# Two transformer layers with routed experts on one core: the routed work cut into 16 tiles of 512 rows and 6 of 256, and the last normalisations dealt out in small steps

## The reference, cut to what matters

```python
x = x + _layernorm(attention_1(_layernorm(x)))               # 8 sequences of 512 rows, 512 columns
y = _layernorm(x)
h = y + attention_2(rmsnorm(y, ln1_w))
z = rmsnorm(h, ln2_w)
shared = (silu(z @ sh_gate) * (z @ sh_up) / 8) @ sh_down     # 512 -> 256 -> 512
probs = sigmoid(z @ router_w + router_b)                     # 7 routed experts
scores, idx = top_k(probs, 2); scores = scores / sum(scores)
combined = sum over e in 0..6 of w[..., e] * expert_ffn(z, r_gate[e], r_up[e], r_down[e])
x = x + _layernorm(h + shared + combined)
```

## Time and profile before

| | us |
|---|---|
| runs (3) | median 2325.95, 2321.92 to 2331.52 |
| the profiled execution's own time | 2323.38 |
| its span, first to last instruction | 2321.6 |
| PE busy / DVE busy / ACT busy / POOL busy | 2116.8 / 1554.4 / 1066.8 / 1064.4 |
| mean granted TensorE clock | 0.962 of full |

### The profile page before, as it was taken

The page is one execution under the profiler, slowest core; times in us unless marked ns, Lnnn a source line. Parts: engine busy times, 40 slices in busy tenths (PEclk is TensorE's granted clock), DMA queues, the critical chain, the costliest instruction groups (busy, mean ns, idle before and its releaser), DMA issues. The chain is left out here.

```text
span 2321.6 us, 38326 instructions
## 1 busy us (share of the span) xinstructions
PE 2116.8 (91%) x12880; PEld 1513.4 (65%) x12880; DVE 1554.4 (67%) x4272; ACT 1066.8 (46%) x2166; POOL 1064.4 (46%) x1092
## 2 busy tenths in 40 slices
PE   5899989999989999998999999897799899999993
PEld 5676565766756667665666766564477788888872
DVE  5766667676666767767676776666475566555557
ACT  2435454434554433455443444544243555555533
POOL 1455555455555354556454554554255233333322
PEclk9999999999989999999999999998899999999997
DMA  5645466654555654565655646335368787778896
GB/s 169 180 121 164 128 164 198 163 151 111 169 151 166 182 154 133 131 178 153 170 169 138 183 132 172 99 99 173 132 241 291 237 196 195 191 199 208 212 269 220
DMA packets 226527, 400.00 MB, mean 172 GB/s; under 512 B 25118, under 2 KB 95646, under 8 KB 222238
## 3 DMA queue, kind: packets, MB, share of 16 engines
q1 hardware_dynamic: 162590, 297.86, 44.4%
q0 software_dynamic: 17792, 39.99, 8.9%
q10 hardware_dynamic: 45952, 59.71, 7.7%
HBM read 147.85 MB, written 148.44 MB: 128 GB/s over the span
## 5 line engine op out<-in xcount | busy, mean ns | idle before, releaser
L1043 DVE CUSTOM_DVE_ANT_0 unused<-score,mask 128x128 bf16<-128x128 f32 (+3 forms) x1024 | 468.0, 486 | 259.5 <-PE score L1279 242.3
L792 ACT ACTIVATE probs<-scoresT 128x512 f32<-128x512 f32 (+3 forms) x1024 | 426.5, 437 | 458.1 <-PE scoresT L1302 443.4
L1302 PE MATMUL scoresT<-stacks 97*128 97x256 f32 (+2 forms) x1024 | 395.4, 400 | 34.8 <-ACT probs L792 26.3
L697 POOL TENSOR_TENSOR probs<-probs 128x1536 f32<-128x1536 f32 (+1 forms) x128 | 374.9, 2929 | 34.2 <-PE out_ps L1316 25.0
L1279 PE MATMUL score<-stacks 96*128 96x256 f32 (+2 forms) x1024 | 349.2, 386 | 20.3 <-DVE rowmax L1043 17.4
L1161 PE MATMUL middle<-weights_by_part,xh 128*128 128x256 f32 x1792 | 343.8, 287 | 6.3 <-DVE weights_by_part L1012 4.6
L2372 PE MATMUL into<-xh,weights_by_part 128*128 128x512 f32 x960 | 330.0, 406 | 7.5 <-DVE acts L2275 3.5
L686 POOL TENSOR_SCALAR_AFFINE_SELECT probs<-probs 128x512 f32<-128x512 f32 x256 | 164.8, 644 | 339.0 <-ACT probs L792 339.0
L1161 PEld LDWEIGHTS middle<-weights_by_part,xh 128*128 128x128 f32 x1792 | 291.2, 192 | 17.1 <-DVE weights_by_part L1012 5.3
L1302 PEld LDWEIGHTS scoresT<-stacks 97*128 97x128 f32 x1024 | 193.3, 192 | 158.3 <-ACT probs L792 93.7
L1279 PEld LDWEIGHTS score<-stacks 96*128 96x128 f32 x1024 | 183.3, 194 | 153.2 <-issue 117.6
(11 more groups left out here) (206 smaller groups left out, 3340.9 us busy)
## 6 DMA issues: line engine op xcount, KB each, us to landing
stacks<-rows SPq DMA_DIRECT2D x768, 128.0 KB, 2.4
x_slots<-mask ACTq DMA_DIRECT2D x56, 1032.0 KB, 5.4
rows<-in_L_attn_x SPq DMA_DIRECT2D x16, 1024.0 KB, 5.8
weights_by_part<-parts_kept SPq DMA_DIRECT2D x7, 2048.0 KB, 8.7
rows<-x_slots SPq DMA_DIRECT2D x12, 1032.0 KB, 7.5
raw<-in_gates SPq DMA_DIRECT2D x24, 512.0 KB, 3.9
raw<-in_ups SPq DMA_DIRECT2D x24, 512.0 KB, 5.0
raw<-in_downs SPq DMA_DIRECT2D x24, 512.0 KB, 5.8
```

Source lines behind the costliest of these rows:

```text
L697: pool.tensor_tensor(probs[0][:, :, P * j:T], probs[0][:, :, P * j:T], probs[j][:, :, :], ALU.add)\
L792: act.activation(probs[j][:, h, 0:width], scoresT[:, u % ST_BANKS, first:first + width], ACT.Exp, scale=SCALE).then_inc(exp_done, 1)
L1043: ins = dve.tensor_tensor_reduce(unused[t][:, :], score.bank(name)[:, first:first + width], mask[:, T - width:T], 1.0, MASKED, ALU.add, AL ...
L1302: pe.matmul(scoresT[:, u % ST_BANKS, 0:T - first], heads[0:ROWMAX + 1, 1, h, j * P:(j + 1) * P], heads[0:ROWMAX + 1, 0, h, first:T], start ...
```

## The change

1. **Tiles.** There are now 16 routed units of 512 rows ("big") and 6 of 256 ("small"), the small ones at places 3, 7, 11, 14, 18 and 21 of the 22. `x_slots` is divided in slots of 256 rows and a big unit loads two. A small unit's gate and up matmuls have 256 columns, its down product has two tiles instead of four, and its `y` and scattering are two instead of four. `make_table` gets 28 instructions instead of 13. One more clearing DMA of 1 MB on the ACT queue stands in the attention layers.
2. **Weights.** Gate, up and down weights wait and are waited for apart (`raw_in[n]`), both where SP loads into `raw` and where the product begins. Among the small units four of the six splits of the following unit's weights stand in the small unit and two in the unit behind it.
3. **x1.** `x1` of the closings 0 to 3 is loaded at the routed units 4, 8, 12 and 16, into buffers that are free there.
4. **Closings.** Six sums are loaded ahead instead of five, the closings are in the order of sequences 0, 1, 5, 2, 3, 6, 4, 7, and their steps stand one by one among the steps of the late units (`among`). POOL adds `x1` to 4, 3, 3, 3, 3, 2, 1, 1 of the four tiles of the closings, 20 of 32 in all; DVE adds the other 12.

```diff
@@ constants and units
-SUMS = 2 + GIVEN
+SUMS = GIVEN + 3
+BY_POOL = (4, 3, 3, 3, 3, 2, 1, 1)
+BIG, SMALL = 16, 6
+SMALL_AT = (3, 7, 11, 14, 18, 21)
+X1_AT = (4, 8, 12, 16)
+        self.tiles = [TT // 2 if k in SMALL_AT else TT for k in range(routed)]
-        return [s for pair in zip(range(EARLY), late) for s in pair] + list(range(len(late), EARLY))
+        return [0, 1, late[0], 2, 3, late[1], 4, late[2]]
@@ expert_order
+        if kind == "routed":
+            yield "LW", n + 2, 0, 2
+        if u + 2 < count:
+            yield "LR", units.opening[u + 2] - blocks
+        if kind == "routed":
+            yield "LW", n + 2, 2, 3
+            if n in X1_AT:
+                yield "LX1", X1_AT.index(n)
+        if u > 0 and units.tiles_in(u - 1) < TT:
+            yield from splits(u - 1, 4, 6)
+            first, second, third = (0, 2), (2, 4), (4, 6)
+        elif small:
+            first, second, third = (0, 1), (1, 3), (3, 4)
+        else:
+            first, second, third = (0, 3), (3, 5), (5, 6)
+    among = {("GU", 0, 1, 1): [("LX1", 6)],
+             ("DN", 0, 1): [*measured(0), ("LA", EARLY)],
+             ("TA", 1, 0): [("CN", 0), *measured(1, 0, 2)],
+             ("FA", 1, 0): measured(1, 2),
+             ("TA", 1, 1): given_out(0),
...
+             ("DN", 2, 1): [*measured(5), *given_out(4), ("CN", 5), ("LA", EARLY + 2), *measured(6), *given_out(5), ("CN", 6),
+                            *measured(7), *given_out(6), ("CN", 7), *given_out(7)]}
@@ SP: weights
-                        sp.wait_ge(split_high, CHUNKS * (i - 1))
-                        sp.wait_ge(split_low, CHUNKS * (i - 1))
+                    for n in range(first, last):
+                        of = (gates, ups, downs)[n]
+                        if i > 1:
+                            sp.wait_ge(split_high, CHUNKS * (i - 2) + 2 * n + 2)
+                            sp.wait_ge(split_low, CHUNKS * (i - 2) + 2 * n + 2)
@@ POOL: scattering and x1
-                    for t in range(TT):
+                    for t in range(units.tiles[k]):
+                def add_x1(m):
+                    pool.wait_ge(*x1_landed(m))
+                    for t in range(TT - BY_POOL[m], TT):
+                        pool.wait_ge(closed, TT * m + t + 1)
+                        pool.tensor_tensor(sums_of(m)[:, t, :], sums_of(m)[:, t, :], x1_of(m)[:, t, :], ALU.add)\
+                            .then_inc(out_ready_pool, 1)
@@ PE
-                            pe.wait_ge(split_low, CHUNKS * i)
+                    if m == 0 and i > 0:
+                        pe.wait_ge(split_low, CHUNKS * (i - 1) + 2 * n + 2)
+                    columns = P * units.tiles_in(u)
-                                       np.s_[:, c, :])
+                                       np.s_[:, c, 0:columns])
-                    for t in range(TT):
-                        if m == 0 and u > 0:
-                            pe.wait_ge(*evacuated(u - 1, t))
+                    if m == 0 and i > 0:
+                        pe.wait_ge(split_low, CHUNKS * i)
+                    for t in range(units.tiles_in(u)):
```

More of the change, by code:

```diff
@@ new lines, in of_unit @@
+    def of_unit(u):
+        kind, n = units.kinds[u]
+        late = n - EARLY if kind == "late" else -1
+        more = u + 1 < count
+        o = units.opening[u + 1] if more else None
+        if kind == "routed":
[6 more added lines that the diff above has]
+                yield "LX1", X1_AT.index(n)
+        yield "OUT", u - 1
+        if late == 0:
+            yield from [("LSM", m) for m in range(SUMS)]
+            yield from [("LX1", 4), ("LX1", 5)]
+        yield "GU", u, 0, 0
+        yield "TA", u, 0
+        if more:
+            yield "XT", o, 0
+        small = units.tiles_in(u) < TT
+        if u > 0 and units.tiles_in(u - 1) < TT:
[5 more added lines that the diff above has]
+            first, second, third = (0, 3), (3, 5), (5, 6)
+        yield from splits(u, *first)
+        yield "GU", u, 0, 1
+        yield "FA", u, 0
+        if more:
+            yield "XT", o, 1
+        yield "AH", u, 0
+        yield from splits(u, *second)
+        yield "GU", u, 1, 0
+        yield "TA", u, 1
+        if more and not small:
+            yield "XT", o, 2
+        yield from splits(u, *third)
+        yield "GU", u, 1, 1
+        yield "FA", u, 1
+        if more and small:
+            yield "XT", o, 2
+        yield "AH", u, 1
+        if more:
+            yield "XT", o, 3
+        if more and units.kinds[u + 1][0] == "routed":
+            yield "EX", n + 1
+        yield "DN", u, 0
+        yield "DN", u, 1
```

450 lines of the change are left out of this document (247 added, 203 removed).

## The result

The changed kernel took 2256.3 us (median of 4, 2252.77 to 2260.6), beside 2325.68 for the kernel before on the same chip (4 runs): a ratio of 0.970, 95% interval [0.9679, 0.9729]. Forecast was 2261, in a range of 2245 to 2281. The profiled execution is the slowest of the four: 2260.6, with a span of 2258.9, 62.7 less than the 2321.6 of before. The medians differ by 69.4, so that the 63 us of the forecast fit the profiled executions better than the medians.

What follows compares the result with a forecast made beforehand. PE was taken to bound the routed stretch and a queue of closings on DVE the end; 46 (small units) + 0 (begin) + 17 (late part) = 63 us off gave 2261, own range 2246 to 2272, with rivals 2245 to 2281.

Steps and rivals of the forecast that it cites:

- Small units, on PE: Six small routed units: 9.0 us less PE work each, 9.5 without waits, taken as 10.6 instead of 18.5.
- the wait for `actl`: In each small unit PE waits about 0.7 us for DVE to write `actl` before the last six matmuls.
- Behind a small unit: Five big units behind small ones: the third pair of splits waits for down weights, 0.3 us each, 1.5 in all.
- DMA: Routed stretch: DMA engines 84% busy against 80%, with scattering at 7.0 and loads at 2.8 us per MB.
- Begin: Begin of the routed units: longer table and earlier ACT start cancel, 0 us, between -2 and +2.
- Late units and the end: First late unit (T0) to the end: T0 + 82.8 instead of 99.9 us, a gain of 17.
- POOL's chain: Late part: from T0 + 28.4 POOL runs seven scales (20.0 us) and 18 additions (23.0) without gaps, setting the end.
- rival (b): Late part stays long: POOL's additions and late sums 6 and 7 cost 4 us per late unit; T0 + 95, 2273; chance 0.12.
- PE's part: Late units: PE runs through without long waits, last matmul near T0 + 54 instead of 69.
- Both engines at once: Late part: DVE's and POOL's additions exclude each other, four times 0.6 us, 2.4 in all, bounds 0 and 7.2.
- (a): Rival: feeding by splits, scattering and loads keeps small units at 14 us, 2280 in all; chance 0.12.
- (c): Rival: breaks in small units lower PE's clock through the following big unit, up to 16 us each, 2357; chance 0.02.

Runs made afterwards that it cites:

- e5: The changed kernel run again with nothing edited, in another set of runs: 2260.33 us, ratio 0.9725 to the kernel before.
- e1: Changed kernel, with the gate and up matmuls of the six small units at 512 columns again: 2300.73 us, ratio 0.984 to the kernel before.
- e7: Changed kernel, with ACT waiting for all three weight matrices of a unit before its first split: 2292.28 us, ratio 0.985 to the kernel before.
- e6: Changed kernel, with the last closing's sums loaded into hsum right behind the store of closing 0: 2260.78 us, ratio 0.9724 to the kernel before.
- e11: e6 with POOL's 20 additions of x1 on 4 columns instead of 512, leaving x1 out of most of those tiles: 2273.56 us, ratio 0.9711.
- e3: Changed kernel, with all 32 additions of x1 on DVE and none on POOL: 2274.45 us, ratio 0.9722 to the kernel before.
- e8: e6 with POOL adding x1 to 4, 3, 3, 3, 1, 1, 0, 0 tiles and DVE taking five more: 2256.19 us, ratio 0.9707 to the kernel before.
- e9: Changed kernel, with the four x1 loads in routed units 2, 6, 10 and 17: 2275.22 us, ratio 0.9708 to the kernel before.
- e2: Changed kernel, with the closings as whole blocks again behind the late units: 2293.0 us, ratio 0.9791 to the kernel before.
- e4: Changed kernel, with x1 of closings 0 to 3 loaded at the begin of the late units: 2280.98 us, ratio 0.9743 to the kernel before.

## Why the prediction was right, point by point

**Small units, on PE: right, with one term too large.** The work that goes was forecast at 9.0 per small unit, less 1.1 of waits and restart, so 7.9. Measured is 7.8 in the small unit itself and 0.9 in the big one ahead of it, 8.6 together: the transpositions of a small unit's rows are done by the unit ahead, where the forecast took them off the small one. That changes the pitches (floor 10.2, not 9.5) but not the sum. What was mis-sized is the wait for `actl`: 0.24, not 0.7, and a restart of some 0.3; the schedule put together by hand had ACT and DVE too slow. That is 0.7 per small unit, 4.4 us more gain. It went again into the first routed unit (1.3), the units behind small ones (0.5 more than forecast) and the later begin (2.6), so that T0 came where it was forecast. That these cancel is luck: in e5 the begin was 5.7 us earlier and T0 was 2170.62. e1 puts the narrow matmuls at 5.3 per unit, for 5.5.

**Behind a small unit: right in kind.** The third split pair waits for down weights: 1.5 us forecast, 2.0 in this execution, up to 5.4 in others. The term that was wrong stands one part further: the x1 loads were costed at nothing, because the gate weights behind them have slack. They do; the down weights ahead of them in SP's queue don't. The runs price that at 2.1 us for three of the four loads.

**DMA: under-sized.** 84% was forecast, 90% measured; in the stretch above the loads took 46.0% and scattering 43.9%, where the earlier trace rows had 39.9 and 39.6. The volume was right: 52.47 MB of loads and 18.35 MB of scattering in 325 us are 85% at the forecast's prices. What was too small is the price of scattering, 7.0 us of all engines per MB, where it is now 325 x 0.439 / 18.35 = 7.8. Down weights took 6.7 us to land for 5.7. With ACT's coarse wait these loads are on PE's path (e7).

**Begin: right within its bounds (0, between -2 and +2).** The table's first and last rows after, beside the earlier trace rows:

```profile
1787.90 0.27 DVE L2313 TENSOR_TENSOR over<-base,steps 128x112 f32<-128x112 f32 x1
...
1792.82 0.29 DVE L2383 CAST table<-tablef 128x44 uint32<-128x44 f32 x1
...
1798.61 1.16 ACT L2100 ACTIVATE weights_by_part<-raw 128x512 fp32r<-128x512 f32 x2 [1.24 <-DMA raw<-in_gates]
1800.52 0.63 ACT L2100 ACTIVATE weights_by_part<-raw 128x512 fp32r<-128x512 f32 x1 [0.76 <-DMA raw<-in_ups]
```

The table takes 5.2 us for 3.1, 2.1 more, where at least 2.5 was forecast. ACT waits 1.24 and 0.76 for 5.29, and PE's 3.70 are gone. What comes back is the clock, the busy times of the first routed unit before and after:

```profile
1812.87:1833.03 20.16, 20.16 (x89) 16.33 (x89) 13.72 (x28) 9.87 (x17) 0.36 (x1) 0.92 0.59 208
1815.49:1836.92 21.43, 21.43 (x88) 17.31 (x89) 13.81 (x28) 9.94 (x17) 0.36 (x1) 0.86 0.72 264
```

PE never stands within this unit, in either kernel, and takes 21.43 us at a mean granted clock of 0.86 for 20.16 at 0.92. That is the 1.3 us that the first routed unit is longer; the forecast had no term for it. The unit with the table and the first routed one together: 47.2 for 47.6, so -0.4, and 46.7 in e5. The 2.6 us by which this execution starts its routed units late are from an early unit (34.4 for 31.9; 32.1 in e5) and from before it (1.7), less 1.7 that the unit with the table gives back. e5, the same kernel on another chip, begins its routed units 3.1 earlier than the kernel before, so the 2.6 is not put down to the change.

**Late units and the end: the sum right (82.8 for 83.2), its terms less so.** POOL's chain in the changed kernel, from the second closing's scale on: the first additions, some of the later ones, and the last scale.

```profile
2204.12 0.23 POOL L2052 TENSOR_SCALAR padded<-meanvar 128x4 f32<-128x4 f32 x1 [8.22 <-DVE meanvar L2458]
...
2206.39 5.50 POOL L2071 TENSOR_TENSOR y<-y,hsum 128x512 f32<-128x512 f32 x4
...
2228.35 4.20 POOL L2071 TENSOR_TENSOR raw<-raw,xl 128x512 f32<-128x512 f32 x3
...
2246.24 0.56 POOL L2052 TENSOR_SCALAR padded<-meanvar 128x4 f32<-128x4 f32 x1
...
2248.59 0.20 POOL L2064 TENSOR_TENSOR shift<-minus_mean,rstd 128x4 f32<-128x4 f32 x1
```

It starts at T0 + 28.4, as forecast; the terms printed for it give 28.4 only if the 0.65 of `xh` is counted within the 3.5, and 29.1 otherwise. Seven scales took 16.8, not 20.0: the 2.86 of the earlier trace rows was a slow one (1.9 to 2.6 here). The 18 additions took 24.0 for 25.4, 23.0 and the 2.4 for both engines at once. Gaps took 4.1 where none was forecast: 2.46 of them from the sum of closing 7, which is the part of rival (b) that was true and which e6 removed. Last scale done at T0 + 73.1, for 73.8; behind it 10.1 us for 9.0. So the sum came right by two errors that cancel, the scales too dear and the gaps left out. Late gaps of POOL, waiting for DVE or a load, were one of the forecast's own signs of being wrong, and they are there.

PE's part was forecast at T0 + 54 and came at 53.6, with no wait and clock 1.00: right.

That POOL's chain is the bound is right only in part: without the work of its additions (e11 against e6) the end comes 5.6 us earlier, and all additions on DVE (e3) give the same end. The queues of POOL and DVE end close together, and easing one finds the other.

**Both engines at once.** 2.4 was put on DVE and POOL excluding each other, four times 0.6. In the changed kernel three of the 18 additions are held up, 1.71 to 1.75 for 1.26 to 1.31, so 1.4 in all. The Trainium skill's rule ("SBUF — State Buffer", section "Who interferes with whom"), that a DVE instruction with two SBUF inputs contends with a GpSimd instruction that reads SBUF, is borne out: with narrow adds, 2.48 and 3.09 become 1.25 and 1.88. In e8 it took 2.0 of the gain (4.05 for three).

**Rivals.** (a) fell with pitches of 10.7. (c) fell: the clock is 1.00 in the routed stretch with PE's breaks of 0.24 to 0.29 us and one of 0.77. Its mechanism is real with longer breaks: in e7, with 4.0 to 5.3 us, the clock fell in each of the five units, for 3.4 to 6.8 us and not for the whole unit that the rival feared. (b) was true only in the late sum of closing 7; PE lost nothing in the late units, and the end is T0 + 83.2, not 95.

## What to carry to other kernels

When one unit of a pipeline gets shorter, ask which transfer is then needed soonest and what is issued right behind it in the same queue: ACT's waiting by part was worth 32 us here, moving the x1 loads by one or two units about 2 us. When a wait of the matrix engine goes, look at the granted clock behind it as well: in the late units that was 5.5 us beside 9.6 of waits. In a queue that waits for stores to land, every later load is late with them; a buffer that is free by then removes the chain. And take a saving off the unit in whose time the work is done, not off the one it belongs to.

## What the runs showed of the hardware

- A transfer of 1024 KB issued 0.43 us behind one of 512 KB in the same queue delays it: in the three units with such a load ACT waits 2.16, 1.94 and 1.49 us for the down weights (e11), without it 0.84, 0.93 and less than 0.2 (e9).
- Additions of DVE and POOL on SBUF operands hold each other up, one instruction at a time: the one that is held takes 1.74 to 1.75 us for 0.63 to 0.82 on DVE, and 1.71 to 1.75 for 1.26 to 1.31 on POOL; the others of the same row are not much longer than alone. One `actl` of DVE took 1.14 for 0.68.
- After a wait of TensorE of 4.0 to 5.3 us (e7), 2.9 to 3.5 us (before, late units) or 6.57 us (e2), the granted clock was 0.50 for 3.4 to 6.8 us; one wait of 3.15 us in e2 left it at 1.00. With no wait over 0.77 us in the changed kernel's routed and late units from the second on it stayed at 1.00.
- POOL's scale of a closing varies from 1.9 to 2.9 us for the same four instructions, with `rstd` at 1.04 to 1.56.
- A store of 1024 KB among loads took 10.6 us to land (2218.53 to 2229.17) and 13.2 in e4; the last two of the changed kernel, with hardly anything else under way, 4.8 and 4.2.
